# A fused attention and feed-forward kernel: the value rows of a quad take one way, through device memory, instead of two

## What is computed

```python
qh, kh, vh = split(layernorm(x) @ Wq), split(ctx @ Wk), split(ctx @ Wv)
dots = einsum('bhid,bhjd->bhij', qh, kh) * 64**-0.5          # masked, causal
out = einsum('bhij,bhjd->bhid', softmax(dots), vh)
x = x + merge(out) @ Wo + bo
x = x + ffn(layernorm(x), w_gate, w_up, w_down)              # ternary weights, 8-bit activations
```

## Time and profile before

| | |
|---|---|
| median of 3 runs | 715.15 us (714.09 to 719.17) |
| the profiled execution | 715.07 us |
| its span, first to last instruction | 713.3 us |
| mean granted clock of PE | 0.981 of full speed |
| period 1, from DVE's bias step to the next | 20.00 us |
| periods 2 to 29, the same way | alternately 20.89 and 20.47 us |
| end of the last `attend` to the end of the span | 22.0 us |

### The profile page before, as it was taken

How to read it: one execution, slowest core, us unless ns; L and a number is a source line. 1 busy time by engine, 2 the same in 40 slices (tenths; PEclk the granted TensorE clock), 3 DMA queues, 4 the chain that set the end, 5 groups by cost and what they waited for, 6 DMA issues and landing times.

```text
span 713.3 us, 19130 instructions
## 1 busy us (share of the span) xinstructions
PE 680.0 (95%) x7314; PEld 459.9 (64%) x7314; DVE 570.5 (80%) x1425; ACT 494.5 (69%) x878; POOL 349.9 (49%) x343
## 2 busy tenths in 40 slices
PE   6999999999999999999999999999999999999842
PEld 5576766667676666766666677666666766665531
DVE  4668888888888888888888888898788879877673
ACT  4768767767876777787677768866776786676431
POOL 0435555463645546364654635465364546535431
PEclk9999999999999999999999999999999999999985
DMA  7033333333533333343443334343443434333231
GB/s 261 14 75 90 83 96 86 86 93 71 116 82 98 89 87 90 72 112 82 105 89 86 90 71 113 76 106 89 90 91 77 103 75 112 75 76 72 64 74 29
DMA packets 72922, 63.31 MB, mean 89 GB/s; under 512 B 44672, under 2 KB 49024, under 8 KB 72832
## 3 DMA queue, kind: packets, MB, share of 16 engines
q1 hardware_dynamic: 72832, 62.09, 36.5%
HBM read 15.91 MB, written 4.19 MB: 28 GB/s over the span
## 4 chain that ended last, share of the span: by engine, by line
PE 91%; issue 3%; POOL 2%; DMA 1%; DVE 1%; SPq 0%; POOLq 0%; DVEq 0%
PE ps_up L411 8%; PE ps_up L304 7%; PE ps_a L433 7%; PE ps_b L502 6%; PE ps_up L293 5%; PE ps_up L294 4%; PE ps_up L295 4%; PE ps_low L304 4%; PE ps_kv L304 4%; PE ps_a L437 4%; PE ps_low L419 3%; PE ps_up L312 2%; PE ps_up L313 2%; PE ps_up L314 2%; PE ps_low L295 2%
## 5 line engine op out<-in xcount | busy, mean ns | idle before, releaser
L555 ACT ACTIVATE vp<-ps_up 128x512 f32<-128x512 f32 x64 | 38.2, 598 | 143.8 <-PE ps_up L304 143.8
L1013 POOL TENSOR_TENSOR prob_up<-prob_up,row_rec 128x512 f32<-128x512 f32 x64 | 66.0, 1052 | 130.7 <-DVE row_rec L818 130.7
L998 POOL TENSOR_TENSOR hid_b<-hid,neg_round 128x512 bf16<-128x512 f32 x64 | 65.3, 1041 | 127.2 <-ACT hid L555 127.2
L1001 POOL TENSOR_TENSOR prob_up<-prob_up,row_max 128x1024 f32<-128x1024 f32 x32 | 61.3, 1915 | 53.1 <-DVE row_max L803 53.1
L796 DVE TENSOR_TENSOR prob_up<-ps_up,bias_up 128x1024 f32<-128x1024 f32 x32 | 39.2, 1225 | 50.2 <-PE ps_up L411 50.2
L555 ACT ACTIVATE kp<-ps_up 128x512 f32<-128x512 f32 x120 | 68.7, 605 | 9.0 <-PE ps_up L295 7.5
L433 PEld LDWEIGHTS ps_a<-vp,prob_t 128*32 128x32 f32 x2048 | 57.1, 110 | 19.5 <-issue 18.5
L555 ACT ACTIVATE prob_t<-ps_b 128x512 f32<-128x512 f32 x96 | 57.1, 595 | 7.9 <-PE ps_b L502 7.9
L433 PE MATMUL ps_a<-vp,prob_t 128*32 128x128 f32 x2048 | 61.8, 273 | 0.7 <-ACT prob_t L555 0.7
L411 PE MATMUL ps_up<-kp,xn_t 128*32 128x256 f32 (+1 forms) x768 | 61.9, 454 | 0.0
L304 PE MATMUL ps_up<-n_w,ct 128*32 128x512 f32 x512 | 60.8, 592 | 0.6 <-DVE prob_up L796 0.6
(11 more groups left out here) (188 smaller groups left out, 1837.1 us busy)
## 6 DMA issues: line engine op xcount, KB each, us to landing
vp<-v_rows SPq DMA_DIRECT2D x512, 64.0 KB, 2.0
ct<-in_ctx_t SPq DMA_DIRECT2D x16, 256.0 KB, 3.1
x_in<-in_x SPq DMA_DIRECT2D x16, 256.0 KB, 3.2
x_res<-in_x SPq DMA_DIRECT2D x16, 256.0 KB, 3.3
out<-x SPq DMA_DIRECT2D x32, 128.0 KB, 2.0
hid_t<-hid_b SPq DMA_TRANSPOSE x64, 2.9
kp<-in_wk SPq DMA_DIRECT2D x2, 256.0 KB, 3.5
kp<-in_wq SPq DMA_DIRECT2D x2, 256.0 KB, 4.4
```

Source lines behind the costliest of these rows:

```text
L555: copy = lambda dst, src, **kw: nc.scalar.activation(dst, src, ACT.Copy, **kw)
L998: p.tensor_tensor(hid_b[:, c, :], hid[:, c, :], neg_round[:].broadcast_to([P, F]), ALU.add).then_inc(hb_ready, 1)
L1001: p.tensor_tensor(prob_up[:], prob_up[:], row_max[0][:].rearrange("p (c h o) -> p c h o", c=1, o=1) .broadcast_to([P, 2, H, R]), ALU.subtr ...
L1013: p.tensor_tensor(prob_up[:, half, :, :], prob_up[:, half, :, :], rows(row_rec[:, 0, :], H, R), ALU.mult).then_inc(normed, 1)
```

## The change

- The second half of V' is no longer made in float32. `v_unit(n, u)`, u = 0..7, makes all of V' as fp32r value units, u // 4 being the half of the keys. `fill_v` with its 16 matmuls goes. All eight units of quad n+1 are made in period n.
- `vp` is filled through device memory. `save_row` writes each unit's 256 KB from `v_rows[u]` (now eight buffers) into a scratch tensor `v_mem[n % 2]`; `load_v` waits for all eight writes and for `attend(n-1)`, then reads the quad's 2 MB into `vp` in one transfer.
- The order of PE is now a list: `FILL` names 16 units, of which 0 to 6 run before the `xq` transposes, 7 after them, 8 and 9 before T0, 10 after it, 11 to 15 between `prob_transposes(n, 1)` and T2.
- x arrives transposed from the host (`xt`); the mean is taken out of Wq (`centre_wq`, once) and 1/sqrt goes into the bias step, which is now `scalar_tensor_tensor`: two instructions of 512 for the up part, one for the low part. `ln1_apply` and `turn` go, `ln1_stats` stays.
- POOL adds `bo` to x a quad at a time, not a group at a time.
- At the start, PE runs three matmuls on zeros before it makes M and one after the first half; the second half of M is made after two key units. N is rounded straight out of PSUM, its low part is made by DVE instead of POOL. In period 0 the eight value units of quad 0 run ahead of the 16 of `FILL`.

```diff
-            def v_tiles(n, b, dst):
-                col = (n % 2 * 4 + 2) * P // 2 + b * R
-                for h4 in range(QB):
-                    t = mm(dst[h4 * R:(h4 + 1) * R, :], ct[n // 2 % 2][:, col:col + R], heads_of(n_w, h4), ...)
+            def v_unit(n, u, dst):
+                par, col = n // 2 % 2, (2 * (n % 2) + u // QB) * P
+                cols = slice(col, col + P)
+                hi, lo = heads_of(n_hi, u % QB), heads_of(n_lo, u % QB)
                 mm(dst, ct_hi[par][:, cols], hi, start=True, stop=False)
                 mm(dst, ct_lo[par][:, cols], hi, start=False, stop=False)
                 mm(dst, ct_hi[par][:, cols], lo, start=False, stop=True).then_inc(rows_ready, 1)
...
-            def move_rows(n, h4):
-                if n:
-                    sp.wait_ge(attn_ready, n)
-                sp.wait_ge(rows_evac, QB * n + h4 + 1)
-                for b in range(QB):
-                    sp.dma_start(vp[h4 * R:(h4 + 1) * R, b, 0, :, :],
-                                 v_rows[h4][b * R:(b + 1) * R, :, :]).then_inc(vp_moved[h4], 16)
+            def save_row(n, u):
+                jh, h4 = u // QB, u % QB
+                dst = v_mem[n % 2, h4 * R:(h4 + 1) * R, :].rearrange("j (b c x) -> c b j x", b=QB, c=2)
+                if n >= 2:
+                    sp.wait_ge(vp_loaded, 16 * (n - 1))
+                sp.wait_ge(rows_evac, V_UNITS * n + u + 1)
+                sp.dma_start(dst[jh], v_rows[u][:, :, :].rearrange("p a e -> p (a e)")).then_inc(rows_saved[u], 16)
+            def load_v(n):
+                for u in range(V_UNITS):
+                    sp.wait_ge(rows_saved[u], 16 * (n + 1))
+                if n:
+                    sp.wait_ge(attn_ready, n)
+                sp.dma_start(vp[:, :, :, :, :].rearrange("p b c a e -> p (b c a e)"), v_mem[n % 2]).then_inc(vp_loaded, 16)
...
+        FILL = "o0 o1 o2 o3 k0 k1 o4 k2 o5 k3 o6 k4 o7 k5 k6 k7"
...
+                for c in range(2):
+                    v.scalar_tensor_tensor(prob_up[:, c, :, :], banks[c].rearrange("p (h j) -> p h j", j=R), rs1[:, 0:1],
+                                           bias_up[:, n:n + 1, c * R:(c + 1) * R].broadcast_to([P, H, R]),
+                                           ALU.mult, ALU.add).then_inc(biased, 1)
...
+            def warm_up(count):
+                for _ in range(count):
+                    mm(ps_u[:, :], zeros[:, 0:P], zeros, start=True, stop=True)
```

More of the change, by code:

```diff
@@ L138, in build @@
         ones_sb = xn2[:, 0, :]
+        zeros = gated[:, 0, :]
         f_sum = st2[:, 0, 0:3]
@@ L184, in build, with fills, evacuated @@
         makes_k = lambda n: live(n) and n // 2 + 1 < GROUPS
-        def ln1_pairs(n):
-            return [m for m in ([2, 3] if n == 0 else [n + 3]) if live(n) and 2 * m < TILES]
+        FILL = "o0 o1 o2 o3 k0 k1 o4 k2 o5 k3 o6 k4 o7 k5 k6 k7"
+        FIRST_FILL = [("v", 0, u) for u in range(V_UNITS)]
+        def fills(n):
+            own = FIRST_FILL if n == 0 else []
+            if makes_k(n):
+                return own + [("kv"[c == "o"], n + (c == "o"), int(u)) for c, u in (w for w in FILL.split())]
+            return own + [("v", n + 1, u) for u in range(V_UNITS) if live(n + 1)]
+        def evacuated(n, i):
+            kind, m, u = fills(n)[i]
+            return (k_evac, H + K_UNITS * m + u + 1) if kind == "k" else (rows_evac, V_UNITS * m + u + 1)
         PERIODS = range(QUADS + 2)
@@ L349, in mean_weights, with fill @@
                 pe.wait_ge(absum_done, 3)
-                pe.wait_ge(const_set, 3)
+                pe.wait_ge(const_set, 4)
                 mm(ps_g[:, 0:3], ones_sb, f_sum, start=True, stop=True).then_inc(mean_ready, 1)
-            def fill_v(n, b):
-                if not live(n):
+            def fill(n, i):
+                i += len(FIRST_FILL) if n == 0 else 0
+                if i >= len(fills(n)):
                     return
[L356 to L363, removed]
@@ new lines, in fill @@
+                if i >= 4:
+                    pe.wait_ge(*evacuated(n, i - 4))
+                elif i < 2:
+                    pe.wait_ge(biased, 3 * n + 2)
+                elif i == 2:
+                    pe.wait_ge(biased, 3 * n + 3)
+                elif n:
+                    pe.wait_ge(*evacuated(n - 1, len(fills(n - 1)) - 1))
+                if kind == "k":
+                    if u == 0 and m % 2 == 0:
+                        pe.wait_ge(ctlo_ready, m // 2 + 2)
+                    k_unit(8 * (m % 2) + u, (m // 2 + 1) % 2, banks[i % 4])
+                else:
+                    v_unit(m, u, banks[i % 4])
@@ L753, in m_low, with n_low @@
                 low_part(m_lo[:, k % 2, half, :], banks[k], m_hi[:, k % 2, half, :], SCALE, m_lo_done)
+            def n_low(k):
+                dve.wait_ge(n_hi_done, k + 1)
+                half = slice(4 * (k // 2), 4 * (k // 2) + 4)
+                low_part(n_lo[:, k % 2, half, :], banks[N_BANK[k]], n_hi[:, k % 2, half, :], 1.0, n_lo_done)
+            centre_wq(0)
             dve.wait_ge(cthi_ready, 1)
             v.tensor_tensor(ct_lo[0][:], ct[0][:], ct_hi[0][:].bitcast(F32), ALU.subtract).then_inc(ctlo_ready, 1)
-            for k in range(4):
-                m_low(k)
-            for m in range(2):
-                ln1_stats(m)
-                ln1_apply(m)
+            m_low(0)
+            m_low(1)
+            centre_wq(1)
+            m_low(2)
+            m_low(3)
+            ln1_stats(0)
             dve.wait_ge(mask_in, 16 * (QB + 1))
@@ L932, in _ @@
                     scale_hid(n - 1)
-                for m in pairs[1:]:
-                    ln1_stats(m)
-                    ln1_apply(m)
                 if n == 0:
```

352 lines of the change are left out of this document (141 added, 211 removed).

## The result

| | before | after |
|---|---|---|
| median of 4 runs each | 714.69 us | 1033.08 us (1032.02 to 1033.91) |
| ratio to before | 1 | 1.443, 95% interval 1.437 to 1.450 |
| profiled execution, span | 713.3 us | 1032.1 us |
| mean granted clock of PE | 0.981 | 0.832 |
| a period, bias step to bias step | 20.89 / 20.47 us | 24 of 31 from 30.2 to 31.0 us, one 40.4 |

What follows compares the result with a forecast made beforehand. PE, 95% busy, was the bound, with a latency loop over DVE, POOL and ACT under a microsecond behind. Gains 2.4 + 0.9 - 0.4 + 2.0 = 4.9 us off 715.07 gave 710.2 us, range 702 to 1115.

Steps and rivals of the forecast that it cites:

- I cost the detour at nothing: V' through device memory: 14.4 us of queue work a quad, hidden within a 20.6 us period with 8 us to spare.
- its own case: Whole kernel: transfers spread over 16 engines, PE's gain mostly becomes waits at xq and T0, 710.2 us; chance 0.40.
- B: Rival, softmax chain: DVE's or POOL's operations move up with PE, so PE's work counts; 685.5 us, chance 0.12.
- C: Rival, small losses: ACT copies or evacuations bind (0.3 us a period), DMA at lower rate; 725 us as middle, chance 0.10.
- A: Rival, save_row: outermost dimension 4 puts writes on four engines, 32 us a quad, 1078 us; chance 0.38.
- The sign that A named: PE waiting for vp before attend, DMA share near a quarter for long stretches, writes landing in over 4 us.
- idle time at T0: First probability transposes: PE waits on POOL's normalisation, 0.4 and 0.7 us.
- bias step, added to the loop: DVE's up part as two scalar_tensor_tensor taking 1.29 us: +0.06 us, bounds 0 and 0.15.
- T0 to the next bias step: PE from the first probability transposes to DVE's next bias step: one unit more, +0.70, giving 8.06 us.
- periods: Pair of periods 0.03 and 0.14 us shorter, to 20.44 / 20.76 us; 2.4 us won over periods 2 to 29.
- first bias step: Start: zero matmuls let key units run at full clock, scores(0) 2.2 us earlier, first bias step at 26.55 us.
- period 30: No keys to make, four units (2.8 us) leave the path behind T0: 2.0 us won, some perhaps lost to clock.

Runs made afterwards that it cites:

- e2: Changed kernel with only the unit writes laid out as 128 consecutive rows, the quad still read in one 2 MB transfer (value rows misordered, output wrong): 720.73 us.
- e1: Changed kernel with each unit written as 128 consecutive rows and the quad read back in eight transfers of 256 KB: 722.92 us, ratio 1.0108.
- e6: e1 with the earlier kernel's tensor_tensor bias step, factor 1/sqrt left out (scores not the reference's): 715.30 us.
- e5: e1 with the 16 units reordered: eight before the xq transposes, four before T0, one after it, three before T2: 703.85 us, ratio 0.986.
- e7: e1 without its four matmuls on zeros at the start: 723.81 us, ratio 1.0136.
- e9: e5 with one of the four units before T0 put directly behind the xq transposes: 690.47 us, ratio 0.9675.

## Why the prediction was wrong, point by point

**The step that failed: "I cost the detour at nothing".** The bytes were right: the forecast had 14.4 us of all 16 engines a quad; in e2, where all 16 carry it, the queue was busy 68.7% of 718.9 us, 15.4 a quad. The divisor was wrong. The prediction saw that `save_row` writes to an outermost dimension of 4, that no row showed such a shape, and what it would mean; then it gave four engines 0.38 and its own case 0.40 (0.62 with B and C, which also have 16 engines), on the ground that "a 64 KB move lands as fast as one could wish". Those moves have 32 rows outermost on both sides: the row says nothing of a shape with 4. The rule of the Trainium skill that the prediction cites spoke for A, nothing measured spoke against it. That is where the weight should have gone. What the runs showed in its place: the writes run on four engines at 101 GB/s, 20.7 us of writing in a quad, and the detour costs 312 us.

**Rival A's sum.** 1078 us against 1033.9 for the profiled execution. `attend(0)` ended at 67.4 instead of 62; the last one at 1010.4, so a quad took 943.0 / 31 = 30.4 us instead of 32; the tail was 21.7 (22). 5.4 - 31 x 1.6 - 0.3 gives the 44 us that A was too high. The writes themselves run at 25.3 GB/s an engine (101 / 4): 524 KB in 20.7 us, where A had 21.5. The other 1.3 us of the cycle lie in A's upper bound of 3.6 us for the rest and its 2.0 for the landing; the runs don't separate them. The sign that A named was the wrong one too: it expected PE to wait for `vp` before `attend`. PE waited in `down`, later in the same period, and once `hid_t` was there `vp` was as well.

**The forecast's own case, as e1 shows it.** 722.68 us in the profiled execution against 710.2. The mechanism was right: at T0 PE starts 0.07 us behind POOL in odd and even periods, at `xq` it waits 0.35 us, where 0.2 to 0.4 was forecast. The idle time at T0 is smaller than the 0.4 and 0.7 us that were forecast: 0.12 and 0.44. The sizes of the terms were not right:

| term | forecast | e1 |
|---|---|---|
| bias step, added to the loop | +0.06 us | +0.24 (e6) |
| T0 to the next bias step | 8.06 us | 8.19 |
| periods | 20.44 / 20.76 us | 20.76 / 21.08 |
| first bias step (28.75 before) | 26.55 us | 27.21 |
| second bias step | 50.4 us | 51.44 |
| period 30 (20.73 before) | 18.73 us | 18.03 |
| from the last bias step to the end (42.3 before) | unchanged | 44.5 |

28 periods x 0.32 = 9.0 us is the larger part. Of the 0.32, 0.18 is the bias step: an instruction with a scalar for each partition and a repeated bias takes 747 ns, not the 688 of the earlier trace rows, and two of them 1.41 us, not 1.29; the low part takes 743 ns instead of 680 (e6). The range of 0 to 0.15 left out what happened. Another 0.13 lies behind T0. From T0 to the start of the scores e1 takes 6.11 us, 0.05 more than forecast; e5 has four units behind T0 and takes 6.73 us to the bias step, e1 has six and takes 8.19, so 0.73 for one, not 0.70. From the start of the scores to the bias step it takes 2.09 us, where the prediction read 2.00 before; e6, with the old bias step, takes 2.10, so the new instruction is not the cause, which stays open.

Period 30 gave back more than forecast, 2.7 us for 2.0. The end took 2.2 us more. PE has no units in period 31, waits 5.64 us for `xq` (1.64 before), and its granted clock falls to 0.50 (1.2 GHz). The `xq` transposes and the last `attend` of e1, then the last `attend` before the change and in e2:

```profile
685.25 0.69 PE L462 MATMUL ps_a<-id_sb,xq 128*128 128x128 f32 x2 [5.64 <-DVE xq L828]
...
694.62 3.36 PE L435 MATMUL ps_a<-vp,prob_t 128*32 128x128 f32 x64 [0.69 <-ACT prob_t L534]
```

```profile
688.43 1.95 PE L433 MATMUL ps_a<-vp,prob_t 128*32 128x128 f32 x64 [0.69 <-ACT prob_t L555]
```

```profile
694.02 1.96 PE L431 MATMUL ps_a<-vp,prob_t 128*32 128x128 f32 x64 [0.69 <-ACT prob_t L530]
```

The windows from 690 to 695, of e1 and of e2 (the clock is the third number from the end):

```profile
690.00:695.00 5.00, 3.54 (x19) 1.95 (x21) 3.35 (x8) 2.44 (x5) 1.04 (x2) 0.50 0.35 72
```

```profile
690.00:695.00 5.00, 3.36 (x50) 2.26 (x54) 3.75 (x7) 2.37 (x4) 1.82 (x2) 1.00 0.09 28
```

The wait of 5.64 us is the same in e2, and so is the work, but there the clock is back at 1.00 by 690, and the time from the last bias step to the end is 41.8 us instead of 44.5. So most of the 2.2 us is the clock, and it is partly luck: e5, e6, e7 and e9 take 43.8 to 44.4. The prediction had named the clock in brackets and given it no number.

**Smaller faults in the prediction.** The forecast case "spans 704 to 717" leaves out its own bound for ACT: 0.3 x 28 = 8.4 us and 2.5 for the bias step above 710 reach past 720. The upper end of 1115 does not follow from a cycle of 33 us either, which gives 1109. And not every transfer at the start went at 390 GB/s: windows of the kernel before from 4 to 10 us show 288 to 319 GB/s at a share near 1. None of this changes the outcome.

**What held.** A unit is 0.70 us where units follow one another, `turn` and the float32 block save what they took: by PE's work alone the prediction had 41.36 - 1.91 = 39.45 us for a pair of periods; e9, where PE is the bound again, has 19.76 + 19.77 = 39.53. Rival B's 685.5 us was thus about the right price of the change without the loop, and e9's 690.5 comes near it; but it needed another order of the units, not operations that move up by themselves. ACT's copies (C) held PE in every period only in e5, where one of them had nothing to hide behind.

**The start.** The first bias step came 1.54 us earlier than before the change in e1, forecast 2.2. Without the matmuls on zeros it came 0.18 us later (e7). Both differences carry the spread of about 1 us between profiles with the same start.

## What to carry to other kernels

Before a transfer is costed in bytes, look at the outermost dimension of both its sides: here 4 instead of 128 rows in one destination made 720.7 us into 1033. In a profile, look for stretches where the DMA share stands at a fixed fraction (0.26, 0.13) while SP's issues grow long and the other transfers land late; the total over the span (64.9%) hides it. And where PE is 95% busy, work taken from it pays only up to the next loop of latencies: put what is left of it before the places where that loop makes PE wait, as e9 does.

## What the runs showed of the hardware that I had not expected

- A shortage of four engines reaches transfers that don't have the shape. The transposes' landing went from 2.5 us (e1) to 8.7, the store's from 7.3 to 11.3. One issue of a write held SP for about 2.2 us (8.59 / 4), against 0.47 in this row of e1 (the medians of a single issue are 2.2 and 0.38):

```profile
670.52 1.87 SPq L246 DMA_DIRECT2D v_mem<-v_rows  x4
```

- The same bytes in reads of 256 KB instead of 2 MB took the queue 599 us (83.1% of 720.8) instead of 494 (68.7% of 718.9), in a nearly equal time. Two things changed at once, the size of a transfer and its rows (2 KB instead of 16 KB; 121985 packets under 8 KB instead of 85632), and no run separates them. In e9 the queue is at 90.8%; it may be the next thing that a faster version meets, which no run tested.
